# Perceiver kernel on one core: the last mixture's outputs by pairs of blocks, six of eight pairs by way of device memory

## The reference, cut to what matters

```
gate_logits = x @ Wg + bg                       # 512 tokens x 8 experts
gate_scores = softmax(gate_logits)
top1 = argmax(gate_scores); top1_weight = gate_scores[top1]
h = silu(x @ W1[top1] + b1[top1])               # 256 -> 1024
o = h @ W2[top1] + b2[top1]                     # 1024 -> 256
x = x + o * top1_weight
```

## Time and profile before

| | us |
|---|---|
| median of 3 runs | 1020.85 |
| lowest, highest | 1019.12, 1021.55 |
| the profiled execution | 1017.08 |
| its span | 1015.4 |
| the mixture's barrier | 911.7 |
| first hidden product | 928.9 |
| last scattering | 1009.9 to 1011.1 |

### The profile page before, as it was taken

How to read it: one execution, slowest core, us unless ns; L and a number is a source line. 1 busy time by engine, 2 the same in 40 slices (tenths; PEclk the granted TensorE clock), 3 DMA queues, 4 the chain that set the end, 5 groups by cost and what they waited for, 6 DMA issues and landing times. The chain is left out here.

```text
span 1015.4 us, 21154 instructions
## 1 busy us (share of the span) xinstructions
PE 974.8 (96%) x8844; PEld 806.2 (79%) x8844; DVE 557.7 (55%) x815; ACT 497.8 (49%) x716; POOL 168.3 (17%) x171
## 2 busy tenths in 40 slices
PE   8999999888799999899999999999999999989997
PEld 7888887756689985699999999999999987466554
DVE  5677777776434345655656564655555633285222
ACT  5777776363576636544454544445454431413221
POOL 2000000012134413102121111111111110320000
PEclk9999999999999999999999999999999999998999
DMA  5211110012122312111111111111130000899990
GB/s 165 74 47 47 47 49 3 19 46 65 42 64 92 93 72 95 42 43 42 43 42 41 41 41 41 41 41 41 41 124 0 1 1 11 279 341 285 292 293 21
DMA packets 55734, 81.42 MB, mean 80 GB/s; under 512 B 5217, under 2 KB 45106, under 8 KB 55666
## 3 DMA queue, kind: packets, MB, share of 16 engines
q1 hardware_dynamic: 55666, 80.43, 25.4%
HBM read 79.89 MB, written 0.52 MB: 79 GB/s over the span
## 5 line engine op out<-in xcount | busy, mean ns | idle before, releaser
L186 PE MATMUL ps<-f_pT_hi,f_cN_hi 128*128 128x256 f32 x512 | 145.4, 284 | 0.0
L186 PE MATMUL ps<-f_pT_hi,f_cN_lo 128*128 128x256 f32 x512 | 144.7, 283 | 0.0
L186 PE MATMUL ps<-f_pT_lo,f_cN_hi 128*128 128x256 f32 x512 | 144.7, 283 | 0.0
L1596 ACT ACTIVATE e_pr<-ps,e_negmax 128x1024 f32<-128x1024 f32 x64 | 71.5, 1118 | 129.9 <-DVE e_negmax L1601 127.6
L1867 DVE TENSOR_TENSOR f_pT_lo<-ps,f_pT_hi 128x1024 fp32r<-128x1024 f32 x64 | 78.3, 1224 | 82.0 <-ACT f_pT_hi L1805 82.0
L186 PE MATMUL ps<-e_cT_hi,e_qb_hi 128*128 128x512 f32 (+1 forms) x288 | 115.0, 399 | 0.0
L186 PE MATMUL ps<-e_cT_hi,e_qb_lo 128*128 128x512 f32 (+1 forms) x288 | 109.7, 381 | 0.0
L186 PE MATMUL ps<-e_cT_lo,e_qb_hi 128*128 128x512 f32 (+1 forms) x288 | 108.9, 378 | 0.0
L1805 ACT CAST f_pT_hi<-ps 128x1024 fp32r<-128x1024 f32 x64 | 65.1, 1017 | 84.7 <-PE ps L1917 84.6
L445 DVE SCALAR_TENSOR_TENSOR a_u<-ps,a_floor,a_cap 128x1024 f32<-128x1024 f32 x64 | 79.2, 1280 | 46.0 <-PE ps L540 45.6
L186 PEld LDWEIGHTS ps<-f_pT_hi,f_cN_hi 128*128 128x128 f32 x512 | 97.8, 191 | 2.6 <-issue 0.8
(11 more groups left out here) (388 smaller groups left out, 1993.2 us busy)
## 6 DMA issues: line engine op xcount, KB each, us to landing
k_w<-in_L_ffn_W SPq DMA_DIRECT2D x30, 1024.0 KB, 14.2
a_ctxT<-in_ctxT SPq DMA_DIRECT2D x16, 512.0 KB, 4.6
d_w<-in_L_ffn_w SPq DMA_DIRECT2D x32, 256.0 KB, 2.7
e_raw<-in_ctxT SPq DMA_DIRECT2D x8, 1024.0 KB, 5.0
e_raw<-in_ctx SPq DMA_DIRECT2D x8, 1024.0 KB, 5.4
k_b<-in_L_ffn_b SPq DMA_DIRECT2D x14, 256.0 KB, 12.3
e_wq<-in_L_xattn_w_q SPq DMA_DIRECT2D x1, 1024.0 KB, 5.1
e_wk<-in_L_xattn_w_k SPq DMA_DIRECT2D x1, 1024.0 KB, 7.7
```

What stands on the lines that cost most here:

```text
L186: last = nc.tensor.matmul(out, a[i], b[j], start=start and n == 0, stop=stop and n == 2, skip_group_check=skip)
L1596: nc.scalar.activation(pr[:, p % NPR, :], core.ps[p % 2][:], ACT.Exp, bias=negmax[:, p:p + 1], accum_out=total[:, p:p + 1]).then_inc(exp_r ...
```

## The change

A new class `Ahead` is made before `xattn1`. It owns the tile of the mixture's first W1 (shared with `xattn1`'s wq, which is read early in that stage), a tile of zeros and a device memory tensor `y_rows` of 1024 rows of 256. In `xattn1`, SyncE behind its last loads issues the load of W1 of block 0 and a store of zeros to the rows of the last two pairs. `prepare_sync` leaves that load out.

In the mixture the order goes by pairs: both hidden steps of pair p, both output steps of pair p-1, both turns of pair p. ScalarE and VectorE follow the same order. Pairs 0 to 5 (`VIA` = 6) are not scattered by TensorE: ScalarE copies their output whole (fp32) to a tile, GpSimd stores it to `y_rows`; when all six are stored, GpSimd issues four indirect loads, each of 128 rows of 1 KB, one row for each token by its slot. VectorE then adds loaded rows times top to x (four operations), and after that makes the lo part of the last pair. Pairs 6 and 7 are scattered as before, with the bias. A token of another pair finds zeros in the one or in the other.

```diff
+class Ahead:
+    SLOTS = 8 * P
+    DIRECT = 2
+    def __init__(self, core, tag, w1_d):
+        self.c, self.w1_d = core, w1_d
+        self.w1 = core.sb(tag + "_w1_0", [P, DC, 8 * P])
+        self.zero = core.sb(tag + "_zero", [P, D])
+        self.y_rows = core.nc.dram_tensor(tag + "_y_rows", (self.SLOTS, D), F32).ap()
...
+    def gpsimd(self):
+        self.c.nc.gpsimd.memset(self.zero[:], 0.0).then_inc(self.zeroed, 1)
+    def sync(self, sp):
+        sp.dma_start(self.w1[:], self.w1_d[0, :, :].rearrange("(c p) f -> p c f", p=P)).then_inc(self.w1_in, 16)
+        sp.wait_ge(self.zeroed, 1)
+        first = self.SLOTS - self.DIRECT * P
+        sp.dma_start(self.y_rows[first:, :].rearrange("(i p) d -> p i d", p=P),
+                     bc(self.zero[:], 1, self.DIRECT)).then_inc(self.zero_out, 16)
...
+            @block.gpsimd
+            def _(pool):
+                g = nc.gpsimd
+                rows = lambda j: bass.IndirectOffsetOnAxis(ap=place32[:, j:j + 1], axis=0)
+                pool.wait_ge(place_ready, 1)
+                pool.wait_ge(early.zero_out, early.ZEROS)
+                for p in range(VIA):
+                    pool.wait_ge(y_hi, p + 1)
+                    g.dma_start(early.y_rows[P * p:P * p + P, :], whole[p % 2]).then_inc(y_out[p % 2], 16)
+                for i in range(2):
+                    pool.wait_ge(y_out[i], 16 * VIA // 2)
+                pool.wait_ge(xs_lo, 1)
+                for j in range(TT):
+                    g.indirect_dma_start(back[:, j, :], None, early.y_rows, rows(j)).then_inc(y_back, 16)
...
                 def high(p):
                     act.wait_ge(y_psum, min(2 * p + 2, NCH))
+                    if p < VIA:
+                        if p >= 2:
+                            act.wait_ge(y_out[p % 2], 16 * (p // 2))
+                        A.copy(whole[p % 2], y_bank[:, 0:D]).then_inc(y_hi, 1)
+                        return
...
+                for p in range(NP):
+                    for n in steps(p):
                         act.wait_ge(h_biased, n + 1)
                         A.activation(h[n % 2][:], h[n % 2][:], ACT.Silu).then_inc(h_ready, 1)
+                    if p >= 1:
+                        high(p - 1)
+                    for n in steps(p):
+                        turned(n)
+                high(NP - 1)
...
+                V.tensor_copy(place32[:], slot[:]).then_inc(place_ready, 1)
...
-                scatter_map(0)
+                for k in range(VIA, NP):
+                    scatter_map(k)
...
+                for p in range(NP):
+                    for n in steps(p):
                         biased(n)
+                    if p > VIA:
+                        low(p - 1)
+                    if p % 2 == 0 and p // 2 + 1 < NG:
+                        gathered(p // 2 + 1)
+                    if p % 2 == 0 and p // 2 + 2 < NG:
+                        gather_map(p // 2 + 2)
+                dve.wait_ge(y_back, 16 * TT)
+                for j in range(TT):
+                    V.scalar_tensor_tensor(x[:, j, :], back[:, j, :], top[:, j:j + 1], x[:, j, :], ALU.mult,
+                                           ALU.add).then_inc(x_via, 1)
+                low(NP - 1)
...
+                for p in range(NP):
+                    for n in steps(p):
                         hidden(n)
+                    if p == 0:
+                        gather(1)
+                    else:
+                        for n in steps(p - 1):
+                            output(n)
+                    for n in steps(p):
+                        turn(n)
+                    if p > VIA:
+                        scatter(p - 1)
+                    if p >= 2 and p % 2 == 0 and p // 2 + 1 < NG:
+                        gather(p // 2 + 1)
+                for n in steps(NP - 1):
+                    output(n)
+                bias()
+                scatter(NP - 1)
```

More of the change, by code:

```diff
@@ L1529, in ffn0, with xattn1 @@
         mixture.run(mlaT, None, finished)
-def xattn1(core, a, finished):
+def xattn1(core, a, finished, early):
     nc = core.nc
@@ L1763, in _ @@
                 sp.dma_start(wo[:], a["L1_xattn_w_o"].rearrange("(h p) o -> p h o", p=P)).then_inc(v_in, 16)
+                early.sync(sp)
             @block.gpsimd
             def _(pool):
+                early.gpsimd()
                 def keys(b):
@@ L2250, in __init__ @@
         sb = lambda name, shape, dt=F32: core.sb(tag + name, shape, dt, ctx)
-        self.w1 = [sb(f"_w1_{i}", [P, DC, self.F]) for i in range(self.EARLY)]
+        self.w1 = [early.w1] + [sb(f"_w1_{i}", [P, DC, self.F]) for i in range(1, self.EARLY)]
         self.w2 = [sb(f"_w2_{i}", [P, self.NF, D]) for i in range(self.EARLY)]
@@ L2263, in __init__ @@
         self.pool_step = sem("pool_step")
-        self.w1_in = [sem(f"w1_{i}_in") for i in range(self.RING)]
+        self.w1_in = [early.w1_in] + [sem(f"w1_{i}_in") for i in range(1, self.RING)]
         self.w2_in = [sem(f"w2_{i}_in") for i in range(self.RING)]
@@ L2340, in run @@
         alone = lambda p: p == NP - 1
+        steps = lambda p: [n for n in (2 * p, 2 * p + 1) if n < NCH]
         with ExitStack() as ctx:
@@ L2367, in run @@
             y = [[sb(f"_y{i}_{n}", [P, D], F32R) for n in ("hi", "lo")] for i in range(2)]
+            whole = [xnT[:, i, 0:D] for i in range(2)]
+            back, place32 = xn, sb("_place32", [P, TT], mybir.dt.uint32)
+            early, VIA = self.early, NP - self.early.DIRECT
+            place_ready, y_out, y_back = sem("place_ready"), [sem("y_out_even"), sem("y_out_odd")], sem("y_back")
             dve_step = sem("dve_step")
@@ L2532, in low @@
                                     ).then_inc(y_lo, 1)
[L2534 to L2537, removed]
+                for p in range(NP):
+                    for n in steps(p):
                         biased(n)
[L2539 to L2545, removed]
+                    if p > VIA:
[9 more added lines that the diff above has]
+                low(NP - 1)
+                dve.wait_ge(x_via, TT)
+                dve.wait_ge(placed, NP - VIA)
                 for j in range(TT):
@@ L2646, in _, with bias, attn1_ffn1 @@
                 last.then_inc(row_psum, 1)
-                for n in range(NCH + 4):
-                    if n < NCH:
-                        hidden(n)
[L2650 to L2666, removed]
+                def bias():
+                    pe.wait_ge(mineT_ready, 1)
+                    pe.wait_ge(self.b_in, 16)
+                    for j in range(TT):
+                        t.matmul(acc(j), mineT[:, j * P:(j + 1) * P], self.b2[:], start=False, stop=False,
+                                 skip_group_check=True)
+                for p in range(NP):
+                    for n in steps(p):
+                        hidden(n)
+                    if p == 0:
[5 more added lines that the diff above has]
+                        turn(n)
+                    if p > VIA:
+                        scatter(p - 1)
[5 more added lines that the diff above has]
+                scatter(NP - 1)
+def attn1_ffn1(core, a, out, early):
     with ExitStack() as ctx:
         norm = Norm(core, "j")
-        mixture = Routed(core, ctx, "k", [a["L1_ffn_" + n] for n in ("Wg", "bg", "W1", "b1", "W2", "b2")], norm, out)
+        mixture = Routed(core, ctx, "k", [a["L1_ffn_" + n] for n in ("Wg", "bg", "W1", "b1", "W2", "b2")], norm, out,
+                         early)
         attn1(core, a, mixture)
@@ L2681, in program @@
         ffn0(core, a)
-        xattn1(core, a, core.retire_sems())
-        attn1_ffn1(core, a, out)
+        finished = core.retire_sems()
+        early = Ahead(core, "k", a["L1_ffn_W1"])
+        xattn1(core, a, finished, early)
+        attn1_ffn1(core, a, out, early)
 def layout(inputs):
```

39 lines of the change are left out of this document (19 added, 20 removed).

## The result

| us | before | after |
|---|---|---|
| median of 4 runs | 1020.18 | 1011.57 |
| lowest, highest | 1019.12, 1021.55 | 1009.36, 1013.08 |
| the profiled execution, its span | 1017.08, 1015.4 | 1011.75, 1009.9 |
| the mixture's barrier | 911.7 | 915.8 |
| first hidden product (F) | 928.89 | 931.71 |

The ratio is 0.9908, interval 0.9881 to 0.9935: 8.6 us less in the medians. The forecast was 1011.9. It started from 1020.85, the median of three of these four runs before; from 1020.18 the same 9.0 give 1011.2.

What follows compares the result with a forecast made beforehand. TensorE was taken to bound the last mixture; its order gains 10.9, the way through memory gives back 1.7, and 9.2 lowered to 9.0 takes the median 1020.85 to 1011.9, range 1007.5 to 1017.5.

Steps and rivals of the forecast that it cites:

- The bound: Last mixture: TensorE, 96% busy, runs almost without a break from 928.89 to 1009.93; time taken out there ends the kernel earlier.
- The sum: TensorE's products in the new order: pair 8.11, last scattering could start at 999.01 instead of 1009.93, 10.92 less.
- rival E: Mixture's output products: each costs 1.88 wherever it stands; 6.9 gained, 1013.9; 17% together with another rival.
- the two readings: TensorE passages: 0.15 owed only where the tiling mode changes, sum 10.9; or every new product pays, 8.8.
- The way through memory: Sixth store and four indirect loads: y back at 998.5, scatter(7) at 1000.74, 1.7 of the 10.9 given back.
- B: GpSimd's issue is costly (g 1.6 to 3), VectorE's wait for the loads ends last; 1017.4 at g 2.36; 16%.
- D: Slower: the loads' wait passes break-even at 3.0 per GpSimd issue; 1025.6 at g 4; 6%.
- g: GpSimd's time for one DMA issue of 128 rows, taken as 1.2, bounded by 0.54 and 2.36.
- A: GpSimd's issue is cheap and the whole way through memory hides: 10.9 gained, 1009.9; 16%.
- The weights: Weight stream with five stores added: last w1 at 987.0, wanted 987.94; last w2 about 990.9, wanted 995.2; both in time.
- That buys nothing: Early load of the first 1 MB weight: takes 3.4 us from the stream, which then idles before the next gate; no gain.
- What follows scatter(7) is as before: After the last scattering starts: its 1.16, four sums and the stores of 2.2 keep their lengths.

Runs made afterwards that it cites:

- the order alone: Against the changed kernel: all eight pairs scattered by TensorE, no stores or indirect loads, pair order and early load kept; 1016.38, ratio 0.9958.
- after_again: The changed kernel measured a second time on another occasion, no edit; median 1011.19, ratio 0.9914.
- after_3: The changed kernel measured a third time on another occasion, no edit; median 1010.05, ratio 0.9906.

## Why the prediction was right

**The bound.** TensorE's order set the end until the last scattering, as the rows said. In S - F the order alone gives 3.9 and the removed scatterings up to 7.1 more; the version with the lo part first gets both.

**The sum.** Free order: 70.12 predicted from F to the last scattering, 70.0 and 70.1 measured when nothing is waited for. The agreement holds two small misses of opposite sign. Pair 7 begins at F + 58.72 instead of 59.05, since a pair takes 8.06 and not 8.11. The scattering behind turns costs 1.19, not 0.95: the prediction took 0.19 off because the product before it was also 128 columns wide, and the 1.14 of the earlier trace rows, where a 64-column product stood before it, is not lowered by that. A gather does come down behind turns (1.90 against 2.09); why a scattering does not stays open. In this sum it counts once; in the order alone it counts seven times and was the miss of that expectation. Outputs side by side took 3.45 against the 3.46 taken, so rival E is out (the 2.1 it took off was a little too much: of the 14 outputs only 12, 1.8 in all, stand ahead of the sixth copy, which sets the end). Of the two readings of the Trainium skill, "TensorEngine Tiling (Array Packing)", section Key Properties, the one by which the drain is owed only where the mode changes fits this case: a hidden pair 3.58, an output pair 3.45, with no price between them.

**The way through memory.** Predicted y back at F + 69.6, measured 69.65, 68.4 and 69.3. The agreement of the first is luck in part: its terms miss by up to 1.05, in both directions, and cancel. From the chain after:

| | predicted | measured |
|---|---|---|
| ScalarE's sixth copy ends, from F | 58.4 | 58.2 |
| step and issue of the store | 1.2 | 0.30 + 0.54 |
| store lands, to the first indirect issue | 3.0 | 4.05 (2.3 to 4.75 in the other executions) |
| four indirect issues, first to last | 3.6 | 3.9 |
| last issue's start to y back | 3.4 | 2.7 (up to 3.4 in others) |
| VectorE's sums, lo part, step | 2.24 | 2.15 |

A direct store is cheaper to issue than taken and an indirect load about as taken, 1.28 with its step against 1.2; the store lands later than taken. The traces show what it lands with. In all ten executions that have a sixth store it landed 0.3 to 0.4 behind the last w2, a load issued 7 to 10 us before it, whether that was early or late (from F, and the wait of the last scattering):

| | last w2 lands | sixth store lands | y back | wait |
|---|---|---|---|---|
| after_again | 60.2 | 60.5 | 68.4 | 0.42 |
| after_3 | 60.8 | 61.3 | 69.3 | 1.36 |
| after | 61.9 | 62.3 | 69.65 | 1.68 |
| every store but the last twice | 62.0 | 62.3 | 69.9 | 1.95 |
| the first weight not ahead | 62.7 | 63.0 | 70.4 | 1.89 |

The lines of after, for the issues of 982.03 and 990.19:
```profile
k_w<-in_L_ffn_W SPq DMA_DIRECT2D x1, 1024.0 KB, 11.6
...
k_y_rows<-xnT POOLq DMA_DIRECT2D x1, 128.0 KB, 3.8
```
So the 3.0 stood for something that is not the store's own: by these rows the store lands when the weight stream ends, and the forecast had that end nearly right in its paragraph on the weights (990.9, which is F + 62.0). Why the store never lands ahead of the load no run shows. B and D needed g above 1.6 and are out; A needed y back 1.7 earlier and came within 0.5 of it in one execution. The Trainium skill, "DMA: Bandwidth & Descriptors", section Anatomy of one DMA, had 2.3 from issue to landing for such a store; here six stores took these times, and the last one 2.0 to 4.5 over the executions, so its figure is near the lower end for this place:
```profile
DMA to landing us min/median/max: 3.8/6.3/7.5
```

**The weights.** Last w1 predicted to land at F + 58.1 with 0.9 in hand; it landed at F + 58.4 with 0.3 in hand in the first profile, at 56.7 and 57.3 in the other two. "That buys nothing" was wrong by half a microsecond. The pause of the stream that the step relied on the earlier trace rows is there after, and behind it the stream is full to the end:
```profile
944.00:946.00 2.00, 2.00 (x20) 1.33 (x17) 0.00 (x0) 0.38 (x2) 0.00 (x0) 1.00 0.28 59
946.60:991.00 44.40, 44.40 (x316) 25.03 (x314) 9.35 (x16) 13.82 (x26) 3.36 (x6) 1.00 1.03 326
```
What it misjudged is how much of a load the pause takes. With the first weight back in the stream, the window 944 to 946 moved 150 GB/s in place of 59, and the next 209 in place of 123: (91 + 86) x 2 us = 0.35 MB of the 1.05 went into the pause there. That is an estimate from one pair of profiles: with the lo part first, where the weight is ahead too, the same windows moved 64 and 168, which makes it 0.25. The rest pushed the loads behind it, up to the last w1.

**What it missed.** "What follows scatter(7) is as before" failed: after 1.68 of idle TensorE the product ran at the 1.2 GHz level and took 2.06 instead of 1.16 (at full clock in the two other profiles of after). The forecast priced the wait, 1.7, but took the place of low(7) as given; it is one of instruction order on VectorE.

**The total.** From F to the end 9.2 less was the sum and 9.0 the forecast. Three profiles gave 8.3, 10.5 and 9.5, and the medians of the three occasions 8.6, 9.1 and 10.8. The right median is owed to a right sum on TensorE, to misses that cancel on the way through memory, and partly to luck in how the early stages fell: they alone move a profiled execution by several microseconds.

## What to carry to other kernels

Price a reordering from the rows of the engine that it frees, but take the length of each product from its own row: a discount for its new neighbour (0.19 here) has to be seen once before it is multiplied. When work is moved off the bound engine on a long way, list that way link by link up to the wait it ends in, and ask of each instruction behind that wait whether it needs it; here one 0.34 us operation in front of the wait instead of behind it was worth 0.4 to 2.6 by the profiles, and 1.5 and 3.2 by the medians, which scatter by as much as 2. Where a small store runs beside a stream of large loads, ask when the stream ends, and not only how long the store takes. Compare two profiles from the first instruction of the changed stage, not by their spans.

## What the runs showed of the hardware

- GpSimd issues an indirect load of 128 rows of 1 KB in 0.94 to 1.04 and begins the next 1.25 to 1.34 after it; a direct store of 128 KB is issued in 0.54 (the first one in 0.81).
- A 128 KB store that meets a stream of 326 GB/s lands 6.3 after its issue in the median, and 2.0 to 4.5 after it where the stream is ending. There it landed 0.3 to 0.4 behind the last 1 MB load, in ten executions of ten.
- TensorE's clock was at 0.50 behind idle times of 1.68 and 3.20, fell within the product behind 1.89 and 1.95, and stayed at 1.00 behind 0.42 and 1.36 and where filler products ran through the wait.
- A scattering of eight products costs 1.14 to 1.19 whether products of 64 or of 128 columns stand before it.
